# A four-layer convolution kernel: interpolation weights formed in SBUF by ScalarE instead of through DRAM, in a new order on every engine

## What is computed

```python
x = x + L0(gn(x))   # conditional convolutions: per-sample weights mixed from 8 experts
x = x + L1(gn(x))   # a selective scan over permuted positions
x = x + L2(gn(x))   # a 3x3 convolution with learnt offsets (deformable)
x = x + L3(gn(x))   # three convolutions, each squared
```

```python
py = hh + ky + dy;  px = ww + kx + dx          # ky, kx = -1, 0, 1
val = v00*wy0*wx0 + v01*wy0*wx1 + v10*wy1*wx0 + v11*wy1*wx1
out = einsum('bckhw,ock->bohw', val, w) + b
```

## Time and profile before

| | |
|---|---|
| timed executions, median of 3 | 1092.51 us |
| the profiled execution | 1081.92 us |
| its span, first to last instruction | 1079.7 us |
| mean granted clock of PE | 0.901 |
| bytes moved by DMA | 123.30 MB |

### The profile page before, as it was taken

The page is one execution under the profiler, slowest core; times in us unless marked ns, Lnnn a source line. Parts: engine busy times, 40 slices in busy tenths (PEclk is TensorE's granted clock), DMA queues, the critical chain, the costliest instruction groups (busy, mean ns, idle before and its releaser), DMA issues.

```text
span 1079.7 us, 19256 instructions
## 1 busy us (share of the span) xinstructions
PE 910.5 (84%) x7176; PEld 628.5 (58%) x7176; DVE 735.6 (68%) x2047; ACT 550.5 (51%) x1155; POOL 356.8 (33%) x320
## 2 busy tenths in 40 slices
PE   4687788898989899999989898979989898875733
PEld 2445556565666575666666566656666665644422
DVE  2566467786868677877778686858687876846332
ACT  1132453756556564747465555637474746361412
POOL 2121423424341515252332425162433434242200
PEclk9685989999989999998989899989999998987766
DMA  9001143352626253534435262525344343526060
GB/s 223 26 19 32 39 130 121 88 167 74 195 58 177 84 155 92 164 103 122 143 85 183 68 181 73 173 63 160 112 129 135 107 151 80 173 61 195 8 200 15
DMA packets 116545, 123.30 MB, mean 114 GB/s; under 512 B 64802, under 2 KB 99750, under 8 KB 116454
## 3 DMA queue, kind: packets, MB, share of 16 engines
q1 hardware_dynamic: 107812, 105.46, 33.5%
q0 software_dynamic: 6144, 13.71, 4.5%
q10 hardware_dynamic: 2498, 2.91, 1.2%
HBM read 84.32 MB, written 37.73 MB: 113 GB/s over the span
## 4 chain that ended last, share of the span: by engine, by line
PE 41%; DVE 23%; ACT 16%; issue 9%; POOL 5%; DMA 4%; SPq 1%; ACTq 0%; POOLq 0%; DVEq 0%
PE ps L620 39%; DVE c_w L1270 6%; ACT L955 3%; ACT y L955 3%; ACT d_pad L955 3%; POOL b_res L1184 2%; DVE b_xf L1278 2%; ACT x L955 2%; DVE x L1278 2%; POOL b_yp L1232 2%; DVE st L1305 2%; ACT c_pad L955 1%; DMA b_yp<-y_turned,b_to 1%; DVE b_md L1270 1%; SPq L1793 1%
## 5 line engine op out<-in xcount | busy, mean ns | idle before, releaser
L1232 POOL DMA_INDIRECT b_yp<-y_turned,b_to x64 | 90.3, 1411 | 285.7 <-DMA y_turned<-b_yt 271.1
L620 PE MATMUL ps<-y,inw 128*128 128x392 f32 x384 | 140.0, 509 | 0.0
L1184 POOL TENSOR_TENSOR rs<-ve,root 128x4 f32<-128x4 f32 x64 | 66.1, 1032 | 218.7 <-DVE ve L1274 218.3
L1305 DVE BATCH_NORM_STATS2 st<-x 128x6 f32<-128x196 f32 x256 | 73.7, 351 | 86.5 <-POOL x L1184 76.0
L620 PE MATMUL ps<-c_w,c_zt 126*64 126x196 f32 x896 | 90.8, 351 | 23.5 <-DMA c_zt<-z_turned 10.3
L1270 DVE TENSOR_TENSOR c_w<-c_w,c_hat 126x1176 f32<-126x1176 f32 (+1 forms) x64 | 97.8, 1581 | 11.1 <-DMA c_w<-hat_turned 11.1
L620 PEld LDWEIGHTS ps<-y,inw 128*128 128x128 f32 x384 | 71.3, 196 | 43.1 <-issue 4.1
L620 PEld LDWEIGHTS ps<-c_w,c_zt 126*64 126x64 f32 x896 | 65.1, 144 | 44.2 <-issue 28.9
L620 PE MATMUL ps<-w,a_S 128*32 128x384 f32 (+2 forms) x1280 | 83.7, 401 | 6.1 <-DVE a_S L1278 5.7
L955 ACT ACT_TABLE_LOAD x50 | 64.2, 1283 | 35.9 <-PE ps L620 35.1
L1206 POOL DMA_INDIRECT x_turned<-b_xt,b_to x64 | 63.1, 986 | 35.1 <-DVE b_xt L1281 20.4
(11 more groups left out here) (201 smaller groups left out, 2073.3 us busy)
## 6 DMA issues: line engine op xcount, KB each, us to landing
c_w<-hat_turned SPq DMA_DIRECT2D x32, 771.8 KB
c_w<-hat_turned SPq DMA_DIRECT2D x32, 578.8 KB
z_turned<-c_z SPq DMA_DIRECT2D x32, 441.0 KB
c_zt<-z_turned SPq DMA_DIRECT2D x16, 882.0 KB
b_xp<-x_turned SPq DMA_DIRECT2D x32, 222.0 KB
x<-in_x SPq DMA_DIRECT2D x32, 196.0 KB, 2.7
y_turned<-b_yt SPq DMA_DIRECT2D x32, 196.0 KB
out<-x SPq DMA_DIRECT2D x32, 196.0 KB
```

The lines of the kernel that those rows point to most:

```text
L620: return nc.tensor.matmul(o, l, r, start=start, stop=stop)
L1184: return nc.gpsimd.tensor_tensor(out=o, in0=x, in1=y, op=op)
L1232: nc.gpsimd.indirect_dma_start(out=YP[:, m, h].rearrange("p b d -> p (b d)"), out_offset=None, in_=y_dram[g % 2], in_offset=bass.IndirectO ...
L1305: last = nc.vector.bn_stats(st[s][:, 2 * c + b, :], x[:, c, b, :])
```

## The change

The x hats no longer go through DRAM. `expand` no longer subtracts the column index in its x half, so the x half of `c_hat` holds the plain place px, copied by ACT; only the y half is made into a hat there. A new step f2 6 on ACT, four parts per group, forms the x hats directly in `c_w`: for each column vx one Abs of 126x196 with the bias -vx, then one Relu over the six or eight columns. Two parts (one per sample) do columns 0 to 5, and two do columns 6 to 13. The first may start once PE has read these columns for the group before (`c_free`, given by step d2 2), the others once `acc` of the group before is complete. DVE's products wait for the Relu (`c_near`) instead of a DMA. The stores of `hat_turned`, the loads of `c_w` and their semaphores are gone.

```diff
-            expand[at + 2, 1, k] = k % 3 - 1 - np.arange(HW)
+            expand[at + 2, 1, k] = k % 3 - 1
...
-    "sync": {"n0": {0: 1}, "ta": {3: 2}, "tb": {22: 2}, "f2": {5: 2, 6: 2}, "d2": {0: 2, 1: 1, 2: 2}, "k3": {5: 1}, "once": {0: 1, 1: 1}},
+    "sync": {"n0": {0: 1}, "ta": {3: 2}, "tb": {22: 2}, "f2": {6: 2}, "d2": {1: 1}, "k3": {5: 1}, "once": {0: 1, 1: 1}},
...
-    "n0": (0, 60897, 121794, 182691, 243588, 304485, 365382, 426279, 487176, 548073, 608970, 669867, 730764,
+    "n0": (0, 56737, 113474, 170211, 226948, 283685, 340422, 397159, 453896, 510633, 567370, 624107, 680844,
...
+                    if part == 2:
+                        last.then_inc(c_free.sem, 1)
                     if part == 6:
                         last.then_inc(H.filled("acc", g), 1)
...
-                    fn(c_hat[b][:, :, :].rearrange("p x n -> p (x n)"), R.tile(("ex", b), g)[0:TV, 0:2 * N], ACT.Abs)\
-                        .then_inc(R.drained(("ex", b), g), 1)
+                    t = R.tile(("ex", b), g)
+                    fn(c_hat[b][:, 0, :], t[0:TV, 0:N], ACT.Abs)
+                    fn(c_hat[b][:, 1, :], t[0:TV, N:2 * N], ACT.Copy).then_inc(R.drained(("ex", b), g), 1)
                 if i == 4:
                     drained(act, ("ex", b), g)
-                    x = c_hat[b][:, :, :]
+                    x = c_hat[b][:, 0, :]
                     fn(x, x, ACT.Relu, scale=-1.0, bias=1.0).then_inc(c_hat_ok.sem, 1)
...
+                if i == 6:
+                    h, b = part // G, part % G
+                    if part == 0:
+                        if first(g):
+                            act.wait_ge(ranked, 1)
+                        else:
+                            act.wait_ge(c_free.sem, c_free.count(g - 1))
+                    if part == G and g:
+                        filled(act, "acc", g - 1, H)
+                    drained(act, ("ex", b), g)
+                    cols = VSPLIT[h]
+                    for vx in range(cols.start, cols.stop):
+                        last = fn(c_w[b][:, vx, :], c_hat[b][:, 1, :], ACT.Abs, bias=-float(vx))
+                    last.then_inc(c_apart.sem, 1)
+                    act.wait_ge(c_apart.sem, c_apart.count(g, part + 1))
+                    x = c_w[b][:, cols, :]
+                    fn(x, x, ACT.Relu, scale=-1.0, bias=1.0).then_inc(c_near.sem, 1)
...
-                    v.wait_ge(*hat_in[b][h].at(g))
+                    v.wait_ge(c_hat_ok.sem, c_hat_ok.count(g, b + 1))
+                    v.wait_ge(c_near.sem, c_near.count(g, part + 1))
                     x = c_w[b][:, VSPLIT[h], :]
                     tt(x, x, c_hat[b][:, 0, :].unsqueeze(1).to_broadcast(x.shape), ALU.mult).then_inc(c_w_ok.sem, 1)
...
             def d2(i, part, g):
-                if i == 0:
-                    load_hats(sp, part, 0, g)
-                if i == 2:
-                    load_hats(sp, part, 1, g)
-                if i == 1:
-                    for m in range(2):
-                        sp.wait_ge(*z_out[m].at(g))
+                if g:
+                    filled(sp, "acc", g - 1, H)
+                for m in range(2):
+                    sp.wait_ge(*z_out[m].at(g))
```

More of the change, by code:

```diff
@@ L220 @@
[L220 to L227, removed]
@@ new lines @@
+    "c0": (0, 56737, 113474, 170211, 226948, 283685, 340422, 397159, 453896, 510633, 567370, 624107, 680844,
+        737581, 794318, 851055),
+    "n1": (0, 56737, 113474, 170211, 226948, 283685, 340422, 397159, 453896, 510633, 567370, 624107, 680844,
+        737581, 794318, 851055),
+    "s1": (0, 56737, 113474, 170211, 226948, 283685, 340422, 397159, 453896, 510633, 567370, 624107, 680844,
+        737581, 794318, 851055),
+    "ta": (0, 56737, 113474, 170211, 226948, 283685, 340422, 397159, 453896, 510633, 567370, 624107, 680844,
+        737581, 794318, 851055),
@@ L250 @@
-        (320075,),
-        (320498, 321619, 326679),
-        (83245, 94720, 140588),
+        (9933,),
+        (59923, 60687, 61656, 66241, 67873, 67873, 80818, 81672, 91824, 105268),
+        (118087,),
+        (122915, 123388, 123661, 129371, 133824, 134510),
+        (137846, 139404, 145735, 153290),
+        (176416, 176416, 177351, 177351, 178200, 178200, 178200, 179897, 180125, 180144),
+        (194292, 194583, 202472, 205298),
+        (222966,),
+        (230668, 230898, 231531, 231531, 231531, 231531, 231531, 231886, 232632, 232677, 236389),
@@ L253 @@
+        (275479, 276222, 276222, 276222, 276222, 278286, 278286, 282541),
+        (287405,),
+        (289216, 293225, 309615),
+        (77690, 113823, 129359),
     ),
     "vector": (
[L255 to L260, removed]
@@ new lines @@
+        (85407, 105130),
+        (108025, 122325, 122769, 122769),
+        (131638, 135546, 142144),
+        (143001, 152181, 155241, 155241, 155241, 160308, 161867, 164762, 164762, 164969, 164969, 165955, 165955,
+        165955, 167345, 168602, 170001, 176149),
+        (187078, 187312),
+        (193077, 193112, 194404),
+        (199738, 210140, 210786, 218604, 226738),
+        (230134, 242419, 242419, 245576, 250991, 251141),
+        (251141, 254570, 256183),
+        (302424, 305630),
@@ L508, in build @@
         y_dram = [nc.dram_tensor(f"y_turned{j}", (HEADS * N, G * HD), F32).ap() for j in range(2)]
-        hat_dram = [nc.dram_tensor(f"hat_turned{j}", (G, TAPS, HW * N), F32).ap() for j in range(2)]
         ps = [ctx.enter_context(nc.psum_tensor(f"ps{i}", [128, 512], F32)) for i in range(8)]
@@ L582, in build @@
         z_in = landed("z_in")
-        hat_out = [landed(f"hat_out{b}") for b in range(G)]
-        hat_in = [[landed(f"hat_in{b}_{h}") for h in range(2)] for b in range(G)]
+        c_apart = sig("distances", 2 * G)
+        c_near = sig("hats_along_row", 2 * G)
+        c_free = sig("c_w_read")
         c_w_ok = sig("c_w", 2 * G)
@@ L600, in drained @@
             eng.wait_ge(ring.drained(f, g), ring.done(f, g))
-        def load_hats(sp, b, h, g):
-            if h == 0:
-                if b == 0 and g:
-                    filled(sp, "acc", g - 1, H)
-                if first(g):
-                    sp.wait_ge(ranked, 1)
-                sp.wait_ge(*hat_out[b].at(g))
-            lo, hi = VSPLIT[h].start * N, VSPLIT[h].stop * N
-            sp.dma_start(c_w[b][:, VSPLIT[h], :].rearrange("p v n -> p (v n)"),
-                          hat_dram[g % 2][b][:, lo:hi].unsqueeze(1).to_broadcast([TAPS, HW, hi - lo]))\
-                .then_inc(hat_in[b][h].sem(g), 16)
         block = ctx.enter_context(nc.Block())
@@ L1757, in f2 @@
             def f2(i, part, g):
[L1758 to L1784 removed]
+                m = part
+                if m == 0 and g > 1:
+                    sp.wait_ge(*z_in.at(g - 2))
+                for k in range(4 * m, 4 * m + 4):
+                    drained(sp, ("z", k), g)
+                sp.dma_start(z_dram[g % 2][:, :, m * HT:(m + 1) * HT, :].rearrange("b t n o -> n b t o"),
+                             c_z[:, m].rearrange("p b (t o) -> p b t o", o=MID)).then_inc(z_out[m].sem(g), 16)
+            def d2(i, part, g):
+                if g:
+                    filled(sp, "acc", g - 1, H)
+                for m in range(2):
+                    sp.wait_ge(*z_out[m].at(g))
+                sp.dma_start(c_zt[:, :, :].rearrange("p b (v o) -> p b v o", o=MID),
+                             z_dram[g % 2].rearrange("b t (y v) o -> (t y) b v o", v=HW)).then_inc(z_in.sem(g), 16)
             def k3(i, part, g):
```

118 lines of the change are left out of this document (43 added, 75 removed), and 2 rows, old and new, of the table PARTS.

## The result

Four timed executions of the changed kernel took 1097.68 to 1106.56 us, median 1102.51; four of the kernel before 1085.93 to 1093.13, median 1090.70. The ratio is 1.0132, with a 95% interval of 1.0071 to 1.0194: slower by 1.3%, 12 us by the medians. The profiled execution took 1101.06 us for a span of 1099.2. (Ratios here leave out executions more than 1.5% above the fastest of their kernel; before's 25 beside the first experiments scatter from 1069.1 to 1108.8 us, so a ratio can lie up to 1.4% above that of the medians.)

A forecast was written before the change was run, and what follows sets the result against it. PE was taken to bound the loop: 58.2 us plus 0.5 for the clock makes 58.7 per group, 1.4 over 57.3; times 15 is 21, less 8 for contention +13, so 1095 profiled, plus 10.6: 1106 us, range 1065 to 1143.

The forecast's parts named there:

- the last step: From profiled execution to median: 1095 us forecast for the profiled one, plus 10.6 us, gives 1106 us.
- The hats' price: ACT's Abs and Relu blocks: 2.78 us per block of six, 3.62 per block of eight, 12.8 us per group.
- The steady group at full clock: One group in the loop: 56.1 + 1.6 + 0.75 - 0.1 - 0.17 = 58.2 us.
- ACT is 2.1 us longer, and PE must wait that long: From PE's expansion to the end of `a_h`: ACT needs 34.5 us, PE 32.4, so PE waits.
- The term of +1.6: PE's wait for ACT's longer stretch up to `a_h`, less 0.55 us of old waits: +1.6 us per group.
- `c_off`: PE waits 0.75 us per group ahead of the expansion for DVE's `c_off`, where it had r1 to do before.
- The clock: Falls of PE's granted clock in the loop: 0.5 us per group instead of 1.2.
- the third rival: The clock falls in every group behind PE's waits, 3.0 us each: 61.2 us per group, 1143 us; chance 0.12.
- Contention: Hat loads delaying the `y_turned` gathers and DVE's product: up to 15.3 us would go; half, 8 us, taken.
- fourth rival: The moved z load collides with the `b_yp` gathers: +1.5 us per group on the forecast, 1129 us; chance 0.08.
- The z exchange: Stores moved ahead of the `y_turned` stores, load behind them: nothing counted, 10 us either way in the range.
- Filling and draining: Stretches before and after the steady loop: left as they were, to 10 us either way.

The follow-up runs named there:

- the first experiments: Changed kernels run after the result; the kernel before, timed again beside them, had medians of 1091.35, 1091.74, 1092.27 and 1095.37 us.
- the group without a fall: One group, 58.3 us, of the changed kernel with three dummy products each ahead of conv1 and the offset convolution; that run: 1078.66 us, ratio 0.9932.
- old order: Changed computation (hats by ACT in SBUF) in the order of the kernel before on every engine: 1086.43 us, ratio 0.9984.
- old order, clock held: Changed computation in the order of the kernel before, with three dummy products ahead of conv1 and four ahead of the offset convolution: 1061.23 us, ratio 0.971.
- the two attempts to mend others: Changed kernel with `d_pad` ahead of `a_pad` and `c_off` ahead of `b_cd`: with the logarithm also moved 1131.51 us, without that 1136.55 us.
- the two mixed kernels: Changed computation in the order of the kernel before: 1086.43 us, ratio 0.9984; before's computation, hats through DRAM, in the changed kernel's order: 1115.29 us.

## Why the prediction was right, and by which errors

The time, 1102.5 against a forecast of 1106, and the mean from the first `c_v` to the last, 58.9 against 58.7 us, were right. Most terms were not; they cancel, and that is luck. So is the last step, which adds 10.6 us for a profiled execution below the median: the changed kernel's was only 1.45 below its own. From profile to profile the change is +19 us, where the sum had +13.

- *The hats' price* was right: 2.77 and 3.62 us per block against 2.78 and 3.62, and (552.3 - 410.1)/12 = 11.8 us more ACT time per group, after what the shorter instructions around it give back. The price of the Relu by columns carried over to Abs; the 15.1 us bound of a bias from SBUF did not come in. The rule of the Trainium skill, "ScalarE: Activation LUTs", section "What ACT_TABLE_LOAD costs", agrees: its immediate form gives 349 ns for 196 columns, the page of the profile 363.
- *The steady group at full clock*, forecast at 58.2 us, came out in its sum: 58.3 in the group without a fall. Its parts were others. The largest new wait, 1.2 us for `c_v`, was put at nothing.
- *"ACT is 2.1 us longer, and PE must wait that long"* is the step that failed. ACT's side came out, 34.6 us from PE's expansion at 379.46 to the end of `a_h` against 34.5. PE's side did not: to the end of the `a_pad` convolution it took 34.05 us, not 31.7 (32.4 with `a_h`). Of the 2.35 us more, 1.34 are its waits for `c_hat` and `d_pad` at the start of that stretch, which stay when the hats are left out; the rest is no wait in the rows shown. So behind the hat blocks PE did not wait for ACT in the new order. In the old one it did, by less than the forecast. The term of +1.6 measures 0.2 (old order), 0.45 (old order, clock held) and, in the new order, 0.9 by the windows or 1.3 by the medians, with next to no waiting in it.
- *`c_off`*, forecast at 0.75, took 0.48 to 0.69. The work ahead of it on DVE, `b_cd`, was at most a small part of the cause; that nothing stands beside it on PE any more is argued, not tested.
- *The clock* had the wrong sign: "a slower PE loses less, so I take 0.5 instead of 1.2". The 1.2 was too small from the start, since the mean of 57.3 us that it comes from holds three draining intervals; over the steady stretch the groups of before lost 58.3 - 56.1 = 2.2 us. In the new order they lose 60.7 - 58.3 = 2.4, by the group without a fall. The falls came in every group, as in the third rival, at a smaller price than its 3.0 us, and most groups had a clock of 0.94, not under its 0.93. The Trainium skill, "Perfetto Trace Analysis", section "Matmul Optimizations", says that products should be run back to back in batches because PE's power follows its use; this trace agrees, with 2.4 us per group lost behind waits of 1.1 to 1.2.
- *Contention*, 8 us to be gained, gave 3 to 5. Without the hat loads `b_yp`'s waits over the whole run fall from 11.1 to 6.1 us in the old order and from 26.5 to 23.5 in the new one, each by one execution. The new order brings more of them than that, so in the changed kernel nothing of it is left. The fourth rival's overlap of `c_zt` with the gathers fits the two groups of 64 us (waits of 1.0 us, then a second fall), but no run showed that it is the load which makes them.
- *The z exchange*, "I count nothing for it": the place of its load is worth 63 us inside the new order, where the old one had a wait of 0.34 us at `b_yp`.
- *Filling and draining*, left at nothing, gave back 5.8 + 3.5 us against the steady stretch. No run took that apart.

What stays open is which of the moves on PE, ACT and DVE makes which of the new waits, that for `c_v` above all; the two attempts to mend others failed.

## What to carry to other kernels

Where an engine bounds a loop, price a wait on it with what its clock does behind it: here two waits of 1.2 and 1.4 us cost up to 3 us per group by the lower clock behind them (59.1 against 56.1 us in the earlier trace rows), and seven throw-away products in them (three took 1.26 us) won 3%, more than either order. When a change is of two kinds (new work on an engine, new order everywhere), build the two mixed kernels first: they showed what the sum could not, that it is the order which costs, and not the move of the hats to ACT. In this ring of PSUM tiles the drains have to stand in the order of the fills, and a small store that others wait for goes ahead of a large load.

## What was not expected of the hardware

ACT, with 46 of 60.7 us of work per group in the new order, 33.6 of them nearly in one piece, made no wait of PE behind the hat blocks. In the old order it made waits of some 1 us per group for `b_xf`, of which 0.2 to 0.45 us were left in the time of a group. The clock fell a second time behind single waits of 1.0 us for `b_yp` in the two groups that start at 489.8 and 553.7. In the other groups that wait was 0.3 to 0.95 us or absent, and the products behind it kept their speed; no run varied it by itself.
